# Attention and expert layer on one core: half-megabyte and weight transfers issued by ScalarE, group turns issued one by one, six more chunks turned by DMA with three row buffers

## What is computed

```python
xn = layernorm(x)                                     # 4096 tokens of 256
scores = (xn @ W_qk) @ xn.T / 16 + (kpos - qpos) * slope   # causal, per batch
s = softmax(scores) @ (xn @ W_v.T)
probs = softmax(xn @ Wr); e = argmax(probs)           # 8 experts, 512 tokens of room each
y[token] = p * (relu(xn[token] @ W1[e]) @ W2[e])      # tokens beyond the room get 0
out = x + s * silu(y)
```

## Time and profile before

| | |
|---|---|
| median of three runs | 438.6 us |
| profiled execution, device time | 441.75 us |
| its span, first to last instruction | 440.0 us |
| TensorE busy | 420.4 us, 96% |
| VectorE busy | 322.4 us, 73% |
| ScalarE, GpSimd busy | 222.7 us, 51%; 228.3 us, 52% |
| TensorE granted clock | 1.00 in all stretches |

### The profile page before, as it was taken

How to read it: one execution, slowest core, us unless ns; L and a number is a source line. 1 busy time by engine, 2 the same in 40 slices (tenths; PEclk the granted TensorE clock), 3 DMA queues, 4 the chain that set the end, 5 groups by cost and what they waited for, 6 DMA issues and landing times.

```text
span 440.0 us, 8367 instructions
## 1 busy us (share of the span) xinstructions
PE 420.4 (96%) x3015; PEld 288.6 (66%) x3015; DVE 322.4 (73%) x838; ACT 222.7 (51%) x444; POOL 228.3 (52%) x353
## 2 busy tenths in 40 slices
PE   6899999998999899999989999999999999999996
PEld 2667576756668676766666666666666666665666
DVE  5989778988888478778747787979796967424553
ACT  3755454452657146545424555545455545454551
POOL 3257851826544826056102566575757576757530
PEclk9999999999999999999999999999999999999999
DMA  7996898366945634266866577676888873234840
GB/s 238 294 294 151 277 295 191 74 130 163 279 90 111 139 115 117 57 216 153 120 96 232 165 245 226 205 250 176 281 156 280 179 206 98 90 120 113 159 98 31
DMA packets 104280, 76.01 MB, mean 173 GB/s; under 512 B 73263, under 2 KB 98108, under 8 KB 102192
## 3 DMA queue, kind: packets, MB, share of 16 engines
q1 hardware_dynamic: 92976, 53.11, 47.3%
q0 software_dynamic: 5824, 16.74, 12.9%
q10 hardware_dynamic: 5440, 5.64, 3.9%
HBM read 31.33 MB, written 28.58 MB: 136 GB/s over the span
## 4 chain that ended last, share of the span: by engine, by line
PE 64%; DVE 13%; DMA 11%; issue 4%; ACT 4%; POOL 1%; SPq 1%; another core or an unknown queue 0%; ACTq 0%; POOLq 0%; DVEq 0%
PE bank L1419 18%; PE bank L1421 18%; PE bank L1420 17%; DMA xg<-in_x 4%; DMA pT<-p_rows 3%; PE bank L1510 3%; DVE sc L1012 3%; PE bank L1513 3%; PE bank L1512 3%; PE bank L1491 2%; ACT sc L1269 2%; DVE p_rows L1033 2%; DMA rows<-xg 1%; DMA slots<-xnr,slot_idx 1%; DMA xeT<-slots 1%
## 5 line engine op out<-in xcount | busy, mean ns | idle before, releaser
L1510 PE MATMUL bank<-v_h,pT 128*128 128x257 f16 x272 | 74.7, 274 | 3.2 <-DMA pT<-p_rows 3.2
L1513 PE MATMUL bank<-v_h,pT 128*128 128x257 f16 x272 | 74.1, 272 | 0.0
L1512 PE MATMUL bank<-v_l,pT 128*128 128x256 f16 x272 | 73.7, 271 | 0.0
L1296 ACT ACTIVATE hid_h<-bank 128x512 f16<-128x512 f32 x64 | 38.1, 596 | 67.7 <-PE bank L1421 59.8
L1102 DVE SCALAR_TENSOR_TENSOR hid_l<-bank,hid_h 128x512 f16<-128x512 f32 x64 | 44.0, 688 | 38.0 <-ACT hid_h L1296 33.7
L1421 PE MATMUL bank<-w_h,hid_l 128*128 128x256 f16 x256 | 69.8, 273 | 0.0
L1419 PE MATMUL bank<-w_h,hid_h 128*128 128x256 f16 x256 | 69.8, 273 | 0.0
L1420 PE MATMUL bank<-w_l,hid_h 128*128 128x256 f16 x256 | 69.8, 273 | 0.0
L1012 DVE CUSTOM_DVE_ANT_0 sc<-bank,bias,score_mul 128x512 f32<-128x512 f32 (+2 forms) x80 | 52.9, 664 | 9.1 <-PE bank L1421 9.0
L1419 PE MATMUL bank<-xT,qT_h 128*128 128x512 f16 (+3 forms) x160 | 55.0, 347 | 3.1 <-DVE cmin L1012 1.7
L1285 ACT ACTIVATE pT<-bank 128x512 f16<-128x512 f32 (+3 forms) x50 | 24.6, 494 | 60.3 <-PE bank L1491 50.9
(11 more groups left out here) (198 smaller groups left out, 919.9 us busy)
## 6 DMA issues: line engine op xcount, KB each, us to landing
raw<-in_w_e SPq DMA_DIRECT2D x5, 2048.0 KB
sc<-in_w_e SPq DMA_DIRECT2D x3, 2048.0 KB
slots<-empty ACTq DMA_DIRECT2D x1, 4224.0 KB, 18.7
gates<-gate SPq DMA_DIRECT2D x8, 512.0 KB
out<-xg SPq DMA_DIRECT2D x7, 512.0 KB
rows<-xg SPq DMA_DIRECT2D x7, 512.0 KB, 7.2
rows<-so SPq DMA_DIRECT2D x7, 512.0 KB
xg<-in_x SPq DMA_DIRECT2D x6, 512.0 KB, 4.4
```

The lines of the kernel that those rows point to most:

```text
L1296: a_.activation(hid_h[:, f % HB, :], sc_ps[f % 2][:, :], ACT.Relu).then_inc(h_hi, 1)
L1510: pe.matmul(pv_ps[t % 2][:, 0:D + 1], p_h, v_h[:, at, q, 0:D + 1], start=kb == 0, stop=False)
L1512: pe.matmul(pv_ps[t % 2][:, 0:D], p_h, v_l[:, at, q, :], start=False, stop=False)
L1513: last = pe.matmul(pv_ps[t % 2][:, 0:D + 1], p_l, v_h[:, at, q, 0:D + 1], start=False, stop=kb == t % NT)
```

## The change

- Transfers: `group_out` of groups 2 to 6, `group_in` of groups 2 to 5, `group_s` of groups 0 to 5 and the first two weight loads leave SyncE's program and are issued by ScalarE, at the end of the steps that `OUT_AT`, `IN_AT`, `S_AT`, `FIRST_LOAD` and `SECOND_LOAD` name. These are 21 transfers.
- Group turns: `turn(g, j)` issues one of the four transposes; `turns_after(t, c)` says after which step. Group 4's move from tile 10 to the steps of tile 11, group 5's from tile 14 to tile 15, group 6's from tile 15 to tile 16, group 7's from tile 20 to tiles 21 and 22.
- `by_dma`: chunks (20,0), (21,0), (22,0), (23,0), (23,1) and (27,0) are turned by DMA too: 36 instead of 30. Three row buffers instead of two; the third lies in `hid_h`. The semaphore is one for each parity of the tile and chunk.
- Units: the last group's `VAL` units move to steps 0 and 1 of tile 23, its `RANK` to the last step of tile 24.
- `next_rows(1)` moves from tile 26 to after the loop.

```diff
-        p_rows = [sb(f"p_rows{k}", [P, GT, 2, P], F16) for k in range(2)]
+        p_rows = [sb(f"p_rows{k}", [P, GT, 2, P], F16) for k in range(NX - 1)]
+        p_rows += [hid_h[:, HB - 2:HB, :].rearrange("p f t -> p (f t)").rearrange("p (b h t) -> p b h t", b=GT, h=2)]
...
-            if t in (REST - 1, TILES - 1):
+            if chunk_blocks(t, c) < GT:
                 return False
-            if chunks(t) == 4:
-                return c == 1 if t == NT - 1 else c in ((1, 2) if t < NT else (0, 1, 2))
-            return chunks(t) == 3 and c < 2
+            if t < NT:
+                return c == 1 if t == NT - 1 else c in {3: (0, 1), 4: (1, 2)}.get(chunks(t), ())
+            return c in {REST - 1: (0,), TILES - 1: ()}.get(t, range(chunks(t)) if t >= NT + GT else ())
...
-                   REST - 5: [VAL, VAL + 1] * last,
-                   REST - 4: [VAL + 2, VAL + 3] * first + [PICK] * (c == 1),
-                   REST - 3: [RANK] * first,
+                   REST - 5: [VAL, VAL + 1] * first + [VAL + 2, VAL + 3] * (c == 1),
+                   REST - 4: [PICK] * (c == 1) + [RANK] * last,
...
+        def turns_after(t, c):
+            if t in (3, 6):
+                return [(t // 3 + 1, j) for j in range(GT) if last_step(t, c)]
+            if t == 11:
+                return [(4, j) for j in range(GT) if min(j, 2) == c]
+            if t in (NT - 1, NT):
+                return [(t - 10, c)]
+            if t in (REST - 7, REST - 6) and c < 2:
+                return [(LATE, (t - REST + 7) * 2 + c)]
+            return []
...
-        SECOND_LOAD = 23
+        FIRST_LOAD, SECOND_LOAD = (6, 0), (23, 1)
+        OUT_AT = {(4, 0): 2, (8, 0): 3, (10, 0): 4, (12, 0): 5, (17, 0): 6}
+        IN_AT = {(5, 1): 2, (9, 0): 3, (11, 1): 4, (13, 2): 5}
+        S_AT = {(6, 1): 0, (9, 2): 1, (13, 0): 2, (18, 0): 3, (21, 1): 4, (25, 1): 5}
...
                 for c in steps(t):
                     if by_dma(t, c):
                         chunk_turn(t, c)
+                    for g, j in turns_after(t, c):
+                        turn(g, j)
...
-                    if i >= 2:
-                        act.wait_ge(pT_in[i % 2], i // 2 * 16)
+                    if dma_no(t, c) >= NX:
+                        b, m = in_rows[dma_no(t, c) - NX]
+                        act.wait_ge(pT_in[b % 2][m], landed(b, m))
...
+            def transfers(t, c):
+                if (t, c) in OUT_AT:
+                    group_out(OUT_AT[t, c])
+                if (t, c) in IN_AT:
+                    group_in(IN_AT[t, c])
+                if (t, c) in S_AT:
+                    group_s(S_AT[t, c])
+                if (t, c) == FIRST_LOAD:
+                    act.dma_start(raw[:, :, :], w_k[0]).then_inc(w_in[1], 16)
+                if (t, c) == SECOND_LOAD:
+                    act.wait_ge(w_lo, 2 * PIECES)
+                    act.dma_start(raw[:, :, :], w_k[1]).then_inc(w_in[1], 16)
```

More of the change, by code:

```diff
@@ L303, in layer_kernel @@
         pT_lo = sem("pT_lo")
-        pT_in = [sem(f"pT_in{k}") for k in range(2)]
+        pT_in = [[sem(f"pT_in{k}_{c}") for c in range(NG)] for k in range(2)]
         pv_full = sem("pv_full")
@@ L374, in dma_no, with landed @@
             return chunk_no(t, c) - turn_no(t, c)
+        in_rows = [(t, c) for t in range(TILES) for c in range(chunks(t)) if by_dma(t, c)]
+        def landed(t, c):
+            return sum(by_dma(k, c) for k in range(t % 2, t + 1, 2)) * 16
         def chunk_cols(t, c):
@@ L385, in row_halves @@
         def row_halves(t, c):
-            k = dma_no(t, c) % 2
+            k = dma_no(t, c) % NX
             return p_rows[k][:, :, 0, :], p_rows[k][:, :, 1, :]
@@ L499, in spread, with turn @@
                 sp.dma_start(wall[:, :], tops[e, 0:2 * P].partition_broadcast(P)).then_inc(w_spread, 16)
-            def turn(g):
+            def turn(g, j):
                 at = key_slot(g // NG, g % NG)
@@ L506, in turn @@
                     sp.wait_ge(score_full, chunk_no(NT, 0))
-                for j in range(GT):
-                    sp.wait_ge(xn_lo, rows_to(g))
-                    sp.dma_start_transpose(xT[:, at, j, :, :], halves[g % NX][:, j, :]).then_inc(xT_in[g % NX], 16)
+                sp.wait_ge(xn_lo, rows_to(g))
+                sp.dma_start_transpose(xT[:, at, j, :, :], halves[g % NX][:, j, :]).then_inc(xT_in[g % NX], 16)
             def rows_of(g):
@@ L547, in chunk_turn @@
             def chunk_turn(t, c):
-                i = dma_no(t, c)
+                k = dma_no(t, c) % NX
                 sp.wait_ge(pT_lo, chunk_no(t, c) + 1)
@@ L552, in chunk_turn @@
                 sp.dma_start_transpose(pT[:, t % 2, c * GT:c * GT + GT, :, :].rearrange("p b h t -> p (b h) t"),
-                                       p_rows[i % 2][:, :, :, :].rearrange("p b h t -> p (b h t)")
-                                       ).then_inc(pT_in[i % 2], 16)
+                                       p_rows[k][:, :, :, :].rearrange("p b h t -> p (b h t)")
+                                       ).then_inc(pT_in[t % 2][c], 16)
             def next_weights(e):
@@ L565, in _ @@
             rows_of(0)
+            group_out(1)
             for t in range(REST):
[L567 to L574, removed]
                 if t == 1:
+                    group_in(1)
                     rows_of(1)
[L577 to L580, removed]
                 for c in steps(t):
@@ L583, in _ @@
                         chunk_turn(t, c)
[L584 to L588, removed]
+                    for g, j in turns_after(t, c):
+                        turn(g, j)
                 if t == FIRST_SCALE - 1:
                     spread(0)
-                if t == SECOND_LOAD:
-                    sp.wait_ge(w_lo, 2 * PIECES)
-                    sp.dma_start(raw[:, :, :], w_k[1]).then_inc(w_in[1], 16)
                 if t == FIRST_ROWS:
@@ L598, in _ @@
                     next_rows(0)
-                    next_rows(1)
+            next_rows(1)
             spread(1)
@@ L1353, in _, with group_out, group_in, group_s @@
                 unit(0, n)
+            def group_out(g):
+                k, n = g % 2, (g // 2 + 1) * 16
+                act.wait_ge(x_in[k], n)
+                act.dma_start(out_g[g], xg[k][:, :, :]).then_inc(out_first[k], 16)
+                act.dma_start(rows_g[g][:, :, 0:D], xg[k][:, :, :]).then_inc(rows_x[k], 16)
+            def group_in(g):
+                k, n = g % 2, (g // 2 + 1) * 16
+                act.wait_ge(xn_made, made_to(g))
+                act.wait_ge(out_first[k], n)
+                act.wait_ge(rows_x[k], n)
+                act.dma_start(xg[k][:, :, :], x_g[g + 2]).then_inc(x_in[k], 16)
+            def group_s(g):
+                act.wait_ge(s_made, g * GT + GT)
+                act.dma_start(rows_g[g][:, :, D:2 * D], so[g % 2][:, :, :]).then_inc(rows_s[g % 2], 16)
+            def transfers(t, c):
[10 more added lines that the diff above has]
+                    act.dma_start(raw[:, :, :], w_k[1]).then_inc(w_in[1], 16)
             def tile(t):
@@ L1373, in tile @@
                             chance(g)
+                    transfers(t, c)
             for t in range(REST):
@@ L1496, in values @@
                 if by_dma(t, c):
-                    i = dma_no(t, c)
-                    pe.wait_ge(pT_in[i % 2], i // 2 * 16 + 16)
+                    pe.wait_ge(pT_in[t % 2][c], landed(t, c))
                 else:
```

## The result

The changed kernel took 450.58 us, the median of four runs (447.43 to 452.79), where the kernel before, beside it, took 438.51 us: a ratio of 1.026, 95% interval 1.020 to 1.0326. On another chip, in six executions, it was 1.0212 (1.0185 to 1.0238). It is slower by 9 to 12 us; 435.6 us was predicted.

What follows compares the result with a forecast made beforehand. TensorE, busy 96% of the span, was taken as the bound. Its path to the experts fell from 221.11 to 219.6 us, gaining 1.5; with 1.5 from the last stage, 438.6 - 3.0 = 435.6 us, range 432.2 to 438.9.

Steps and rivals of the forecast that it cites:

- the cases given 8 in 100: The changed kernel measurably slower than the kernel before, beyond about 0.5%: chance 0.08.
- the path along TensorE: TensorE's own work and waits up to the experts, summed to 219.6 us against 221.11, deciding over the router's 219.3.
- part 2: Spreading the transposes of groups 4 and 5 ends TensorE's waits on late chunk turns: gain 3.2 us (0 to 3.2).
- Part 1: Six turns of 0.43 us each leave TensorE, all ahead of the experts: gain 2.6 us.
- Part 3, (21,0): The new DMA turn of (21,0) misses its use by TensorE: 1.3 us late (0 to 2.0).
- Part 4, (23,1): The turn of (23,1), beside the second load, lands near 197.0 when TensorE wants it at 193.2: 3.8 us late (0 to 3.8).
- Part 4, (25,0): The turn of (25,0), beside group 5's result transfer, lands late: 1.0 us (0 to 1.5).
- Part 4, ScalarE's queue: Issuing 21 transfers at 0.52 us each costs 0.2 us in tile 4 (0 to 1.0) and 0.1 around tile 10.
- Part 5: A third row buffer ends waits in the last stage: gain 1.5 us (0.5 to 1.5).
- (A): All turns land in time and the router's chain rules: 433.5 to 432.5 us, chance 0.20.
- (B): The router's chain gives the gain back, TensorE resuming near 221, only the last stage gains: 437.1 us, chance 0.22.
- (C): Turns starve beside ScalarE's transfers in tiles 8 to 10 and 24 to 26: slower, 441.6 us, chance 0.10.

Runs made afterwards that it cites:

- the base: The kernel before with only the third row buffer and the semaphores of the change: 437.83 us, 0.9983 of the kernel before.
- one part alone: Only the six more DMA turns added to the base, all transfers and group turns on SyncE as before: 446.72 us, 1.0171.
- a part alone: Only the transfers moved to ScalarE on top of the base: 437.63 us, 0.9981.

## Why the prediction was wrong

The sign was wrong; it lay in the cases given 8 in 100. The step that failed is the path along TensorE, which the sum had at the first expert matmul at 219.6 us and which was there at 228.08. The 8.5 us by terms, from the profile after: 2.1 for the late turns of part 2 that stayed (0.67 at (11,0), 1.45 at (15,1)); 2.3 at tile 13 and 1.6 at `RANK`, which had no term; 1.3 more at (21,0) and 0.5 more at (23,1); 1.5 of work for the clock, which had none either; less 1.8 for three terms that did not come (0.5 for group 7's keys, 1.0 for (25,0), 0.3 for ScalarE's issues). Some 1.0 is left over and not placed. Of the other 3.15 us between that profile and the median some 2.2 are, by the estimate above, the lower clocks of the other executions (0.990 against 0.995).

The start was off as well. The gain of 1.5 us was taken from the 221.11 of one execution, which lay 3.15 us over the median and had a wait for `xeT`; the base's profile, with the same order of work up to there, has 218.06. Against that the sum's own 219.6 is a loss of 1.5. By its steps:

**Part 1, six turns off TensorE, -2.6.** The 24 transposes went. What they saved was more than given back by the landings: the six turns alone cost 8.9 us.

**Part 2, group turns apart, -3.2, and the counts, -0.8.** Half right: the wait at (11,0) fell from 1.82 us to 0.67. The one at (15,1) did not go, and its cause seems to be another (last section). Overlooked was what else is in SyncE's queue behind the group turn: `tops<-wmax`, the router's transfer. It was issued at 101.62 instead of 99.90 and met ScalarE's 1 MB of `group_out(5)`:

```profile
101.07 0.38 ACTq L1363 DMA_DIRECT2D out<-xg  x1
101.49 0.55 ACTq L1364 DMA_DIRECT2D rows<-xg  x1
101.62 0.58 SPq L521 DMA_DIRECT2D tops<-wmax  x1
108.67 0.33 SPq L523 DMA_DIRECT2D gate<-tops  x1
111.70 0.42 DVE L1079 TENSOR_REDUCE wtop<-gate 128x2 f32<-128x256 f32 x1 [5.10 <-DMA gate<-tops]
```

It landed after 7.03 us, where it took 3.2 before; VectorE stood 5.10 us, and TensorE 2.34 at tile 13. Here ScalarE's transfers do harm together with the group turns. With the group turns alone the write lands in 2.7 us, and TensorE waits 1.1 at tile 13; with the transfers alone it lands in 3.3 (the read behind it, `gate<-tops`, in 5.8) and VectorE stands 1.3, TensorE not at all. The counts' wait went, but with `VAL` units straight ahead of `RANK` there is one of 1.6 us for their values in its place.

**Part 3, (21,0), +1.3.** Right place, size off: measured 2.6 in the changed kernel, 3.9 in one part alone. What failed is the landing: 3.20 us was taken from a turn with nothing around it, but this one had group 5's scatters and a result transfer beside it and took 4.6 to 5.5. (22,0) and group 7's keys cost nothing that shows.

**Part 4, (23,1), 3.8 late.** The mechanism was right, the size, 4.31, in part by luck. The sum had the turn land 6.7 us after its issue and TensorE ask for it 2.9 after; measured were 8.91 and 4.65, as TensorE itself came later. The load landed 9.5 us after its issue, at 202.0, and the turn, issued 1.5 us behind it, at 202.9. The Trainium skill, "DMA: Bandwidth & Descriptors", section on queues, rings and completion order, has each DMA engine serve the queues that have work for it in rotation, packet by packet. By that rule a turn in small packets, 0.25 KB each against the load's 7.7 by the queues' rows (if these are the packets meant), would end with the load or behind it, and the trace agrees.

The sentence that the delay "costs almost nothing extra, as the router's chain would hold TensorE anyway" was wrong too, though no part of the 8.5 us hangs on it, as the 3.8 stood in TensorE's path in full. In the changed kernel TensorE never waits for `xeT`, and without the turns of tiles 20 to 23 it does not either and is at the experts at 222.40: the delay was not hidden.

**Part 4, (25,0), 1.0 late.** It did not come: the turn, issued at 210.32, 1.6 us behind the result transfer, landed after 3.1 us, and behind (23,1) TensorE waits for no turn up to the experts.

**Part 4, ScalarE's queue.** Right in the median, shown by a part alone: 0.9981 against 0.9983. In half of the profiles tile 4 cost 0.7 us more than before, within the 0 to 1.0 given for it; the clock that can fall behind it had no term.

**Part 5, third buffer, -1.5.** Right in the profile of the last stage (0.4 us of waits instead of 1.5); in the time 0.7 us, which its interval cannot tell from nothing.

**The rivals.** (A) and (B) fell: there was neither landing in time nor a chain to give time back. (C) named the deciding point, a landing over 4.5 us, and the mechanism, turns that starve beside large transfers, but put it in tiles 8 to 10 and 24 to 26, where most chunks had room, and blamed ScalarE's queue. Most of the harm came at tiles 21 and 23, where the new turns themselves lie.

## What to carry to other kernels

Price a DMA turn by its landing beside its worst neighbour (4.6 to 10.3 us here), not by the one alone (3.2), and ask whether that fits between the last write and the first use; in this kernel the chunks turned by TensorE next to a large load were the slot that let the load through. Idle time of TensorE is dearer than its length when it runs to several us, so a wait that another chain seems to hide still has to be checked for the clock behind it. And a wait seen in one profiled execution that lies above the median of the runs should not carry a step of the sum.

## What the runs showed of the hardware

**The late turn at (15,1).** It landed after 4.45 us before, and the group turn ahead of it was blamed. It lands after 4.5 to 5.2 us in all the other profiles too, group 5's turn ahead of it or not. The DMA view of the kernel before from 141 to 145.6 us, in 40 slices (busy tenths), then its queues:

```profile
DMA  0000000000299999999999650000000079999000
...
q1 hardware_dynamic: 1600, 0.39, 81.7%
q8 instruction: 1, 0.02, 1.3%
```

The transposes stop for eight slices, about 0.9 us, and go on; within the stretch lies one packet of the instruction queue. With group 4's turns apart, where it landed after 5.19 us, the stop is some 1.5 us, again with one such packet. That the engines stood still for this fetch fits, but no run took it away, so it is not shown.

**The clock after a gap.** Stretches at half clock of 3.4 or 6.8 us came in or behind every idle gap of 3.8, 3.9, 4.3, 4.4, 4.5 and 6.3 us in these profiles. Behind gaps of 2.0 to 2.6 us some executions had one and others, of the same kernel too, had none. Which of the short gaps brings it is open. The gap of 3.1 us at the very start has none in any profile.
